# Second attention: the row maxima's lead over the scores is changed from twelve units to eleven

## The reference, cut to what matters

```python
x = x + attn1(layernorm(x))          # x: 2 batches of 1024 tokens, 128 wide

def attn1(x, W_qkv, b_qkv, W_proj, b_proj):
    q, k, v = split(x @ W_qkv + b_qkv)             # 16 heads of 8
    bias = slopes[:, None, None] * minimum(j - i, 0)
    scores = einsum('bhtd,bhsd->bhts', q, k) / sqrt(8) + bias
    w = softmax(scores, axis=-1)                   # 1024 x 1024 for each of 32 batch-heads
    return einsum('bhts,bhsd->bhtd', w, v) @ W_proj + b_proj
```

## Time and profile before

| | |
|---|---|
| median of 3 runs | 1283.65 us |
| profiled execution | 1279.4 us, of it span 1277.5 us |
| PE, DVE, ACT, POOL busy, share of the span | 89%, 66%, 55%, 41% |
| second attention, up to its last score matmuls | about 680 to 1082 us |
| its loop of units with chunks | about 724 to 1056 us |

### The profile page before, as it was taken

How to read it: one execution, slowest core, us unless ns; L and a number is a source line. 1 busy time by engine, 2 the same in 40 slices (tenths; PEclk the granted TensorE clock), 3 DMA queues, 4 the chain that set the end, 5 groups by cost and what they waited for, 6 DMA issues and landing times. The chain is left out here.

```text
span 1277.5 us, 19317 instructions
## 1 busy us (share of the span) xinstructions
PE 1134.9 (89%) x6321; PEld 558.7 (44%) x6321; DVE 847.2 (66%) x1855; ACT 703.5 (55%) x883; POOL 524.5 (41%) x548
## 2 busy tenths in 40 slices
PE   4799999999999997858997599999999999668883
PEld 2444444444444674447973122222222223347773
DVE  6466567567567466833325999999999993683331
ACT  3777777777777534302225267777677777422220
POOL 0066566566566500356852013312311321026774
PEclk9999999999999996968999599999999999798897
DMA  3001010011010103315755431222122110414562
GB/s 97 1 7 25 18 40 23 17 40 23 17 40 18 36 17 106 96 41 155 182 96 111 83 64 44 58 53 64 35 67 59 44 33 1 136 34 97 155 166 21
DMA packets 64825, 77.18 MB, mean 60 GB/s; under 512 B 22856, under 2 KB 49356, under 8 KB 64140
## 3 DMA queue, kind: packets, MB, share of 16 engines
q1 hardware_dynamic: 50312, 66.91, 19.6%
q0 software_dynamic: 11520, 9.18, 5.0%
q10 hardware_dynamic: 2920, 0.16, 0.2%
HBM read 52.46 MB, written 9.83 MB: 49 GB/s over the span
## 5 line engine op out<-in xcount | busy, mean ns | idle before, releaser
L1709 ACT ACTIVATE at_PR<-psum 128x1024 f32<-128x1024 f32 x256 | 248.0, 1021 | 123.1 <-PE psum L1938 122.9
L1777 DVE TENSOR_REDUCE at_MX<-psum 128x1 f32<-128x512 f32 x468 | 301.2, 686 | 10.7 <-PE psum L1920 6.4
L1646 POOL TENSOR_TENSOR at_PR<-at_PR,at_FAC 128x512 f32<-128x512 f32 x64 | 81.2, 1268 | 293.4 <-ACT at_PR L1709 293.4
L486 ACT ACTIVATE PR<-psum 128x1024 f32<-128x1024 f32 x144 | 140.9, 1026 | 82.2 <-PE psum L770 75.3
L491 ACT ACTIVATE PR<-PR 128x1024 f32<-128x1024 f32 x144 | 144.6, 1062 | 0.0
L770 PE MATMUL psum<-Q,K 64*128 64x512 f32 (+3 forms) x768 | 143.5, 502 | 1.2 <-ACT PR L486 1.2
L782 PE MATMUL psum<-PR,V 128*64 128x512 f32 (+3 forms) x768 | 139.7, 495 | 0.1
L1938 PE MATMUL psum<-at_QS,at_KS 122*128 122x512 bf16 x512 | 136.0, 387 | 2.0 <-DVE at_MX L1773 1.6
L1956 PE MATMUL psum<-at_PR,at_VG 128*32 128x512 f32 x1024 | 137.0, 608 | 0.0
L1340 PE MATMUL psum<-moe_XGT,moe_WE 128*128 128x256 f32 x512 | 123.8, 398 | 7.5 <-ACT moe_XGT L1102 7.5
L1218 DVE TENSOR_TENSOR moe_H<-moe_GL,psum 128x512 f32<-128x512 f32 x64 | 43.9, 687 | 125.1 <-ACT moe_GL L1106 95.7
(11 more groups left out here) (232 smaller groups left out, 1613.2 us busy)
## 6 DMA issues: line engine op xcount, KB each, us to landing
moe_WE<-in_c_We SPq DMA_DIRECT2D x32, 768.0 KB
XB<-at_r_dram SPq DMA_DIRECT2D x32, 256.0 KB, 3.8
at_QS<-at_SPL SPq DMA_DIRECT2D x72, 64.0 KB
at_KS<-at_SPL SPq DMA_DIRECT2D x72, 64.0 KB
at_KS<-in_c_krows SPq DMA_DIRECT2D x8, 384.0 KB
moe_rows_dram<-XNS SPq DMA_DIRECT2D x2, 1152.0 KB, 11.9
at_KM<-in_c_max_krows SPq DMA_DIRECT2D x16, 128.0 KB
at_QM<-at_SPL SPq DMA_DIRECT2D x64, 32.0 KB
```

Source lines behind the costliest of these rows:

```text
L486: act.activation(PR[u][:, :, :], S[(b + u) % 2][:, :, :], ACT.Tanh, scale=SCALE0 / CLAMP).then_inc(z.clamped, 1)
L1646: pool.tensor_tensor(pr, pr, FAC[:, 4 * (s // 2):4 * (s // 2) + 4, :], ALU.mult).then_inc(z.factored, 1)
L1709: act.activation(PR[:, gu % PRS, 2 * r:2 * r + 2, :].rearrange("p h n -> p (h n)"), g.psum[:, 2 * r * BANK:(2 * r + 2) * BANK], ACT.Exp).t ...
L1777: dve.tensor_reduce(MX[:, 4 * (2 * pair + c % 2) + I % 4, khalf:khalf + 1], bank(("max", c))[:, :], AX, ALU.max).then_inc(z.reduced, 1)
```

## The change

One constant is changed.

```diff
 PRS = 4
 
-LEAD = 12
+LEAD = 11
 
 FIRST_OUT, SECOND_OUT = 117, 124
```

## The result

The changed kernel takes 1292.21 us in the median of 7 runs (1289.62 to 1296.46), the kernel before 1283.65 (7 runs, 1276.22 to 1287.14). The ratio is 1.0084 with a 95% interval of [1.0061, 1.0107]: slower by 0.8%, and the whole interval lies above 1. The profiled execution takes 1291.28 us with a span of 1289.4, so 11.9 us more than before.

A forecast was written before the change was run, and what follows sets the result against it. VectorE's pace bounds the loop, with TensorE having almost nothing in hand. Waits of +14.6 us, +1.2 at the start and -1.2 at the end sum to +14.6, giving 1294.0 or 1298.3 by base; forecast 1297 us, range 1286 to 1304.

The forecast's parts named there:

- What bounds the loop: Second attention's loop: VectorE sets the pace, 22.42 us per half; TensorE has 0.04 us of slack, so its standstills idle VectorE.
- The absorbed wait: Loop: VectorE's finished banks outlast the standstill, 1279.4 to 1283.7 us, or half absorbed, 1290; chance 0.12 for both.
- The main term: Loop: scores wait for the row's DMAs in 14 halves, 1.04 us each, +14.6 us; at the longest landing 18.8.
- The start: Start of the loop: VectorE's first single chunks come later, +1.2 us, between -1 and +3 depending on the clock's rise.
- The end: End of the loop: the outputs are turned right behind the last split, -1.2 us, between 0 and -2.1.
- The sum: Whole change: 14.6 + 1.2 - 1.2 = +14.6 us.
- this level: Whole kernel: base time between the profiled 1279.4 us and the median 1283.65, giving 1294.0 or 1298.3; uncertain by a few us.
- The chances: Whole kernel: slower by over 1% (12.8 us) 0.64, within 1% 0.35, faster by over 1% 0.01.
- The fallen clock: Loop, rival: each wait drops the granted clock for a unit, 1.24 us more each, 17 in all, 1314 us; chance 0.06.

The follow-up runs named there:

- e5: Changed kernel with SP issuing the first of a row's two DMAs behind the cast alone, not the whole split; ratio to the kernel before 1.0079.
- e2: Changed kernel, lead still eleven, with each half's row transposed and split two chunks earlier; ratio to the kernel before 0.9990.
- e1: Changed kernel with the lead back at twelve and each half's row transposed, split and copied four chunks later; ratio to the kernel before 1.0144.
- e4: The changed kernel itself, unedited, timed a second time on one chip with other runs; ratio to the kernel before 1.0114.
- e10: e2 once more, with no further edit; one execution, no ratio, stage 417.7 us.
- e11: Changed kernel with the edits of e2 and e5 together; ratio to the kernel before 0.9968.
- e6: Changed kernel with a lead of ten, 40 wide chunks and the first turn of the outputs one unit later; ratio to the kernel before 1.0657.
- e9: e2 with SP's 384 KB copy issued behind the small stack copies; ratio to the kernel before 0.9975.

## Why the prediction was right, point by point

- **What bounds the loop.** Right. A standstill of TensorE at the scores makes VectorE idle for as long (1.19 and 1.19 us in half 2), and e5 shows 0.31 us for 0.31 us. The absorbed wait, the rival to which I gave 0.12, needed slack that is not there. With the row early enough the wait and the longer period both go (e2), and with the lead left at twelve they come back with the late row (e1).
- **The main term.** Right in mechanism, count and place: waits at halves 1 to 14, none at 15. Its size was 14 x 1.04 = 14.6 us, and 16.3 was measured, 1.16 each. The missing 0.12 us is made up of small things: the landing takes 1.74 to 1.75 us where I worked with the rounded 1.7, the second DMA starts 0.62 us behind the first and not 0.60, and TensorE starts 0.04 to 0.09 us behind the landing, for which I had set only the 0.04 us of slack. The Trainium skill's page "DMA: Bandwidth & Descriptors" (section "Anatomy of one DMA — SWDGE (gpsimd) path") gives about 2.0 us of fixed cost for a DMA of the GpSimd path, by which the term would be 18.8, an estimate. The row read from the trace, an SP DMA's, was the better guide.
- **The start.** Wrong in sign: -0.5 us instead of +1.2. The first part was as forecast, VectorE starts 1.35 us later; but the clock rose 3.8 us sooner after the first scores, which I had only as a bound of the term (-1). e4 repeats it. That the moved scores caused it is not shown, since in e10 and e11 the rise came another 5 us sooner with the same order.
- **The end.** Right: -1.1 us at the turn of the outputs, where -1.2 stood.
- **The sum.** +14.6 us forecast, +14.6 measured from the first scores to those of unit 120. That it fits so well is partly luck, since the main term was 1.7 us too small and the start 1.7 too large.
- **From the sum to the time.** The span grew by 11.9 us and not by 14.6. The stage began 1.9 us earlier in the execution profiled after, and it took 35.0 us instead of 36.2 from the scores of unit 120 to its end, where its last 6 us ran at a clock of 0.94 instead of 0.67; what follows the stage took 0.5 more. The prediction held this level uncertain by a few us. It gave 1297 us, and 1292.21 was measured, inside 1286 to 1304. Against the median of before that is 8.6 us, where the forecast had 13; in the second comparison it was 12.7.
- **The chances.** I gave 0.64 to slower by over 1%. The ratio of the first comparison, 1.0084, is within 1%, that of the second, 1.0114, beyond it, and the intervals of both contain 1.01. The loss seems to lie at the very border: the stage's 13.3 us are 1.0% of 1283.65. As the centre was 1.8 us above the border, 0.64 was a little too sure.
- **The fallen clock.** It did not come at standstills of 1.1 us, for which I had given it 0.06, and came at 3.8 us in e6, with 1.4 to 2.9 us per half where the rival had set 1.24 for a unit.

## What to carry to other kernels

When work that runs ahead is moved closer to its use, look for the longest chain of small steps between the two (here transpose, split, two DMA issues, a landing: 4.1 us from the transpose to the scores), count how many units of the loop stand between its ends, and subtract. Here nothing was lost while the rows landed before the scores came up. What they were late was lost in full, every time round, because the two busiest engines are coupled through three buffers. The remedy lies in the chain and not in the lead: made earlier, the row allows the shorter lead, which then gives 2.0 us in the loop's tail, too little for the ratios here to tell it from a lead of twelve with the same row. And leave the chain more than its usual time, since a landing now and then took about twice as long.

## What the runs showed of the hardware that was not expected

- A small DMA from SP (4 KB) lands 1.7 us after the start of its issue nearly always, but after 2.2 to 3.7 us where a packet of the instruction queue q8 starts 0.5 to 2.4 us behind the split (ten rows in five kernels), in e2, e9 and e10 in the same two halves. No run takes the packet away.
- TensorE started 0.04 to 0.09 us after the landing it had waited for (after, all 14 waits).
- At a standstill of TensorE of 3.8 us the granted clock fell (0.62 in the 3.2 us behind that of half 2), 14 times in a loop, and the period grew by 2 us on average on top of the wait; with standstills of 1.1 us in the same loop it stayed at 1.00.
- The clock rose from 0.50 some 13 us after the loop's first scores before and 9 us after. With a lead of twelve it was 12 to 13 us in four traces, with eleven 9 to 10 in five and 4 in two. The order of the start may play a part, but the same kernel (e2, e10) had it at 9.7 and at 4.0.
